# Attention with causal softmax, one core: weighted sums taken one key tile at a time, and part of the softmax denominators added up by VectorE

## What is computed

```
q = (x @ Wq.T + bq).reshape(b, l, h, hd).transpose(0, 2, 1, 3)      # k and v alike
scores = jnp.einsum('bhqd,bhkd->bhqk', q, k) / math.sqrt(hd)
scores = jnp.where(causal, scores, -jnp.inf)
att = jax.nn.softmax(scores, axis=-1)
out = jnp.einsum('bhqk,bhkd->bhqd', att, v)
return out.transpose(0, 2, 1, 3).reshape(b, l, d) @ Wo.T + bo
```

## Time and profile before

| what | value |
|---|---|
| median of 3 runs | 2973.25 us (2972.68 to 2973.93) |
| the profiled execution: its own time, and its span | 2975.39 us, 2972.8 us |
| TensorE busy, whole span | 2809.0 us (94%) |
| weight loads busy | 2017.9 us (68%) |
| VectorE busy | 1477.6 us (50%) |
| ScalarE busy | 1050.1 us (35%) |
| GpSimd busy | 1282.0 us (43%) |

### The profile page before, as it was taken

The page is one execution under the profiler, slowest core; times in us unless marked ns, Lnnn a source line. Parts: engine busy times, 40 slices in busy tenths (PEclk is TensorE's granted clock), DMA queues, the critical chain, the costliest instruction groups (busy, mean ns, idle before and its releaser), DMA issues. The chain is left out here.

```text
span 2972.8 us, 42529 instructions
## 1 busy us (share of the span) xinstructions
PE 2809.0 (94%) x16692; PEld 2017.9 (68%) x16692; DVE 1477.6 (50%) x3069; ACT 1050.1 (35%) x1446; POOL 1282.0 (43%) x672
## 2 busy tenths in 40 slices
PE   4999999999999999799999999999999968999998
PEld 2888888888888888555555555555555536888886
DVE  4232223222312222366666666666666626777775
ACT  1322321131213111255555555555555541212121
POOL 2322332242225111367777777777777741212110
PEclk8999999999999999799999999999999988999998
DMA  7444343333336544445455545555545235454541
GB/s 245 168 165 165 136 180 130 114 139 145 135 140 192 185 171 164 122 103 117 118 118 119 116 112 118 115 117 119 117 115 118 73 119 159 129 169 128 168 126 61
DMA packets 153999, 404.91 MB, mean 136 GB/s; under 512 B 21820, under 2 KB 57076, under 8 KB 152776
## 3 DMA queue, kind: packets, MB, share of 16 engines
q1 hardware_dynamic: 123480, 292.05, 28.9%
q10 hardware_dynamic: 30320, 110.15, 16.6%
HBM read 270.41 MB, written 131.20 MB: 135 GB/s over the span
## 5 line engine op out<-in xcount | busy, mean ns | idle before, releaser
L1087 ACT ACTIVATE prob<-ps_s 128x1024 f32<-128x1024 f32 (+3 forms) x768 | 598.5, 812 | 474.2 <-PE ps_s L1206 393.3
L787 PE MATMUL ps_u<-h_hi,w_hi 128*128 128x512 f32 x1536 | 611.9, 398 | 2.0 <-POOL h_lo L555 2.0
L787 PE MATMUL ps_u<-h_lo,w_hi 128*128 128x512 f32 x1536 | 600.7, 391 | 0.0
L787 PE MATMUL ps_u<-h_hi,w_lo 128*128 128x512 f32 x1536 | 599.5, 390 | 0.0
L1043 POOL TENSOR_TENSOR added<-added,prob 128x2048 f32<-128x2048 f32 (+1 forms) x128 | 550.0, 4297 | 10.7 <-ACT prob L1087 10.5
L549 POOL TENSOR_TENSOR w_lo<-w_raw,w_hi 128x1024 fp32r<-128x1024 f32 x93 | 222.7, 2395 | 473.0 <-ACT w_hi L617 473.0
L678 DVE SCALAR_TENSOR_TENSOR qk_lo<-ps_u,bias_col,qk_hi 128x512 fp32r<-128x512 f32 x128 | 96.0, 750 | 578.9 <-ACT qk_hi L593 578.9
L1130 DVE TENSOR_REDUCE part_high<-ps_r 128x1 f32<-128x512 f32 x496 | 329.9, 686 | 85.7 <-PE ps_r L1176 77.8
L1126 DVE CUSTOM_DVE_ANT_0 ps_r<-ps_r,row_mask 128x384 f32<-128x384 f32 (+1 forms) x500 | 309.1, 632 | 81.1 <-PE ps_r L1176 69.2
L1176 PE MATMUL ps_r<-k_st,q_st 96*128 96x512 f32 (+1 forms) x1008 | 323.3, 374 | 18.8 <-DMA v_sb<-v_tok 9.0
L787 PEld LDWEIGHTS ps_u<-h_lo,w_hi 128*128 128x128 f32 x1536 | 288.7, 188 | 61.9
(11 more groups left out here) (193 smaller groups left out, 3417.3 us busy)
## 6 DMA issues: line engine op xcount, KB each, us to landing
w_raw<-w_cols SPq DMA_DIRECT2D x72, 512.0 KB, 6.3
qk_split<-qk_hi SPq DMA_DIRECT2D x64, 512.0 KB, 2.6
qk_split<-qk_lo SPq DMA_DIRECT2D x64, 512.0 KB, 4.0
q_st<-qk_split ACTq DMA_DIRECT2D x60, 512.0 KB, 7.6
k_st<-qk_split ACTq DMA_DIRECT2D x60, 512.0 KB, 13.7
xn<-in_L_attn_x SPq DMA_DIRECT2D x8, 2048.0 KB, 12.8
v_tok<-v_out SPq DMA_DIRECT2D x32, 512.0 KB, 4.4
wm<-in_L_wmod SPq DMA_DIRECT2D x8, 2048.0 KB, 8.0
```

What stands on the lines that cost most here:

```text
L787: last = nc.tensor.matmul(ps_u[u % 2][:], w[:, m, k], h[:, k, tok], start=k == 0 and j == 0, stop=k == KT - 1 and j == 2)
L1087: nc.scalar.activation(prob[:, buffer_of(t, k), 2 * pair:2 * pair + 2, off:], ps_s[pair][:, :, off:], ACT.Exp, scale=SCALE).then_inc(exp_d ...
```

## The change

There are four parts.

1. `weigh` takes one step k instead of two. In the slots 2 to 5 the first step of the pair now stands behind the second pair of scores (`rest(t, p, 0)`), and the second at the end of the slot (`rest(t, p, 1)`). In slot 0 the steps 8 and 9 of the block before stand in the middle and `sum_high` at the end; in slot 1 the steps 10 and 11 and then `sum_low` stand at the end.
2. DVE adds the low half's steps into `low_total`, three instructions to a block (`add_low`), behind the second, fourth and sixth of its rows (`LOW_AT`). `sum_low` multiplies `low_total` (384 columns) and the first 128 columns of step 8 by ones.
3. `added` is one buffer instead of two. POOL's first add of a block waits for `sum_high` of the block before and for that block's three `low_added`.
4. ACT copies `ps_o` out before the first exponents of the next block, and the low half's before its sum. `SHARE` goes from (2, 2, 1, 1, 1) to (2, 1, 2, 1, 1).

```diff
-    SHARE = (2, 2, 1, 1, 1)
+    SHARE = (2, 1, 2, 1, 1)
...
                 if k == 1:
-                    if t > 1:
-                        pool.wait_ge(sum_done, sums_upto["sum", t - 2, 1])
+                    if t > 0:
+                        pool.wait_ge(sum_done, sums_upto["sum", t - 1, 1])
+                        pool.wait_ge(low_added, LOW_ADDS * t)
...
+            def add_low(t, i):
+                k = LONG + 1 + i
+                if i == 0:
+                    if t > 0:
+                        dve.wait_ge(sum_done, sums_upto["sum", t - 1, 0])
+                else:
+                    dve.wait_ge(low_added, LOW_ADDS * t + i)
+                dve.wait_ge(masked, masked_upto(t, k))
+                cols = slice(offset(k), BANK)
+                so_far = prob[:, buffer_of(t, LONG), :, cols] if i == 0 else low_total[:, :, cols]
+                nc.vector.tensor_tensor(low_total[:, :, cols], so_far, prob[:, buffer_of(t, k), :, cols], ALU.add).then_inc(low_added, 1)
...
-                pe.wait_ge(masked, masked_upto(t, NSTEP - 1))
-                for k in range(LONG, NSTEP):
-                    off = offset(k)
+                pe.wait_ge(masked, masked_upto(t, LONG))
+                pe.wait_ge(low_added, LOW_ADDS * (t + 1))
+                for total, cols in ((low_total[:], slice(P, BANK)), (prob[:, buffer_of(t, LONG)], slice(0, P))):
...
+            def rest(t, p, half):
+                if p >= HOPS:
+                    weigh(t, 2 * (p - HOPS) + half)
+                elif t > 0 and (p, half) == (0, 0):
+                    weigh(t - 1, LONG)
+                    weigh(t - 1, LONG + 1)
+                elif t > 0 and (p, half) == (0, 1):
+                    sum_high(t - 1)
+                elif t > 0 and (p, half) == (1, 1):
+                    weigh(t - 1, LONG + 2)
+                    weigh(t - 1, LONG + 3)
+                    sum_low(t - 1)
...
                         scores(t, 2 * p + n // 2, n % 2)
+                        if n == 1:
+                            rest(t, p, 0)
                     pass_1(turns[4])
-                    if p >= HOPS:
-                        weigh(t, p - HOPS)
-                    elif t > 0:
-                        (sum_high if p == 0 else sum_low)(t - 1)
-                        weigh(t - 1, PAIRS - HOPS + p)
+                    rest(t, p, 1)
```

More of the change, by code:

```diff
@@ L927, in attend @@
         prob = sb("prob", [P, PBUF, HG, BANK])
-        added = [sb(f"added{i}", [P, HG, BANK]) for i in range(2)]
+        added = sb("added", [P, HG, BANK])
+        low_total = sb("low_total", [P, HG, BANK])
         ones = sb("ones", [P, HD])
@@ L943, in attend @@
         added_up, sum_done, sum_copied = sem("added_up"), sem("sum_done"), sem("sum_copied")
+        low_added = sem("low_added")
         att_stored = [sem(f"att_stored{i}") for i in range(QC)]
@@ L1029, in add @@
             def add(t, k):
-                total, off = added[t % 2], offset(k)
+                total, off = added, offset(k)
                 if k < FIRST:
@@ L1078, in exponents @@
                 if before >= 0:
-                    act.wait_ge(weighed, before // 2 + 1)
+                    act.wait_ge(weighed, before + 1)
                     kb = before % NSTEP
@@ L1154, in _ @@
                             max_all(use[1])
+                    if t > 0 and n in LOW_AT:
+                        add_low(t - 1, LOW_AT.index(n))
+                for i, n in enumerate(LOW_AT):
+                    if t > 0 and n >= len(strewn(t)):
+                        add_low(t - 1, i)
+            for i in range(LOW_ADDS):
+                add_low(NG - 1, i)
         @block.tensor
@@ L1208, in scores, with weigh @@
                 last.then_inc(score_done, 1)
-            def weigh(t, p):
-                if 2 * p == 0 and t > 0:
+            def weigh(t, k):
+                if k == 0 and t > 0:
                     pe.wait_ge(o_copied, 2 * t)
-                if 2 * p == 0 and t == 0:
+                if k == 0 and t == 0:
                     pe.wait_ge(qkv_loaded[0], loads_upto(0))
-                if 2 * p == LONG:
+                if k == LONG:
                     pe.wait_ge(o_copied, 2 * t + 1)
-                if 2 * p < FIRST:
-                    pe.wait_ge(exp_done, 2 * (NSTEP * t + 2 * p + 2))
-                else:
-                    pe.wait_ge(masked, masked_upto(t, 2 * p + 1))
-                for k in (2 * p, 2 * p + 1):
-                    ch, j = steps[k]
-                    off, end = offset(k), j == (ch + 1) * CT - 1
-                    for h in range(HG):
-                        part = slice(h * HD, (h + 1) * HD)
-                        last = nc.tensor.matmul(ps_o[part, off:], v_sb[t % SLOTS][:, j, part], prob[:, buffer_of(t, k), h, off:], start=j == 0, stop=end)
+                if k < FIRST:
+                    pe.wait_ge(exp_done, 2 * (NSTEP * t + k + 1))
+                else:
+                    pe.wait_ge(masked, masked_upto(t, k))
+                ch, j = steps[k]
+                off, end = offset(k), j == (ch + 1) * CT - 1
+                for h in range(HG):
+                    part = slice(h * HD, (h + 1) * HD)
+                    last = nc.tensor.matmul(ps_o[part, off:], v_sb[t % SLOTS][:, j, part], prob[:, buffer_of(t, k), h, off:], start=j == 0, stop=end)
                 last.then_inc(weighed, 1)
                 if end:
-                    pe.wait_ge(weighed, PAIRS * t + p + 1)
+                    pe.wait_ge(weighed, NSTEP * t + k + 1)
                     pe.sem_inc(o_done, 1)
@@ L1236, in sum_low @@
                 bank_free(use)
-                pe.wait_ge(masked, masked_upto(t, NSTEP - 1))
-                for k in range(LONG, NSTEP):
-                    off = offset(k)
+                pe.wait_ge(masked, masked_upto(t, LONG))
+                pe.wait_ge(low_added, LOW_ADDS * (t + 1))
+                for total, cols in ((low_total[:], slice(P, BANK)), (prob[:, buffer_of(t, LONG)], slice(0, P))):
                     for h in range(HG):
-                        last = nc.tensor.matmul(bank_of(use)[h * HD:(h + 1) * HD, off:], ones[:], prob[:, buffer_of(t, k), h, off:], start=k == LONG, stop=k == NSTEP - 1)
+                        last = nc.tensor.matmul(bank_of(use)[h * HD:(h + 1) * HD, cols], ones[:], total[:, h, cols], start=cols.start > 0, stop=cols.start == 0)
                 last.then_inc(sum_done, 1)
@@ L1249, in sum_high @@
                 for h in range(HG):
-                    nc.tensor.matmul(bank_of(use)[h * HD:(h + 1) * HD, :], ones[:], added[t % 2][:, h], start=True, stop=False)
+                    nc.tensor.matmul(bank_of(use)[h * HD:(h + 1) * HD, :], ones[:], added[:, h], start=True, stop=False)
                 for k in range(ADDS + 1, LONG):
@@ L1269, in _ @@
                         scores(t, 2 * p + n // 2, n % 2)
+                        if n == 1:
+                            rest(t, p, 0)
                     pass_1(turns[4])
-                    if p >= HOPS:
-                        weigh(t, p - HOPS)
-                    elif t > 0:
-                        (sum_high if p == 0 else sum_low)(t - 1)
-                        weigh(t - 1, PAIRS - HOPS + p)
-            for p in range(PAIRS - HOPS, PAIRS):
-                (sum_low if p == PAIRS - 1 else sum_high)(NG - 1)
-                weigh(NG - 1, p)
+                    rest(t, p, 1)
+            weigh(NG - 1, LONG)
+            weigh(NG - 1, LONG + 1)
+            sum_high(NG - 1)
+            weigh(NG - 1, LONG + 2)
+            weigh(NG - 1, LONG + 3)
+            sum_low(NG - 1)
 def finish(nc, s):
```

15 lines of the change are left out of this document (8 added, 7 removed).

## The result

The changed kernel takes 2954.26 us (median of 4 runs, 2951.61 to 2954.96), the kernel before 2973.59 us beside it (2972.68 to 2974.79): ratio 0.9931, 95% interval 0.9918 to 0.9944. The direction is as forecast, and the time lies in the range. But 19 us were gained where 46 were forecast.

The account below looks back on a forecast made before the run. TensorE was taken as the bound, busy 35.5 of 36.7 us a block but losing waits to ACT and DVE. The terms summed to -1.50 us a block, -46 us over 31 blocks, so 2927 us; range 2888 to 2965.

Parts of the forecast that it names:

- the fifth: DVE's adds in slot 0 delay the bank `sum_high` needs: new wait 0.65 us a block, ends 0 and 3.
- Two rows of 0.5: DVE's two rows between first and second add in slot 0, reckoned at 0.5 us each, ending at 4.35 us.
- Step 1: The low half's sum on TensorE shrinks from 2.18 to 0.88 us: gain 1.30 us a block.
- Step 2: Five more 32-column groups on TensorE cost 1.5 us a block; its own-matmul wait ahead of `sum_low` adds 0.1.
- step 3: TensorE's scores wait less for ACT's exponents: about 2.0 us a block recovered, ends 0.8 and 3.1.
- step 4: TensorE's waits for DVE outside slot 0: 0.45 of some 0.7 us a block recovered, ends 0 and 0.7.
- Step 6: POOL's first add moves from 5.7 to about 7.9 us into the block, covered by 2.96 us of POOL idling.
- the third rival: DVE adds meeting POOL adds choke the rows: +1.0 us a block, 3004 us; chance 0.11.
- the second: Rival: width changes eat the gain, only 0.8 to 1.3 us of waits recovered; 2955 to 2980 us, chance 0.18.
- The first: Rival: waits vanish almost whole, slot 2 too, none at `sum_high`; -2.9 us a block, 2883 us; chance 0.14.

Follow-up runs that it names:

- order alone: The changed kernel without DVE's adds and with the low half's sum over all four steps as before: 2966.29 us, ratio 0.9975.
- no adds: The changed kernel without DVE's three adds, `sum_low` reading step 8 alone for all 512 columns: 2926.55 us, ratio 0.9845.
- with pairs: The changed kernel with adds behind DVE's rows 2, 5 and 7, and pairs of steps again in slots 2 to 5: 2926.22 us, ratio 0.9839.
- the first experiment: The kernel before with only DVE's adds and the short low sum; order, pairs of steps, `SHARE` and ACT's copies as before: 2998.28 us, ratio 1.0082.
- sum-first order: The changed kernel with adds behind rows 2, 5 and 7, and `sum_low` ahead of the weighted sums of steps 10 and 11: 2937.56 us, ratio 0.9875.

## Why the forecast was right in direction and wrong in size

The forecast's sum and what was measured, in us to a block. Two kernels lie on the way from before to changed (order alone, then no adds, which has the shorter sum as well), so the measured terms add up to the whole difference:

| step | forecast | measured | from the table of slots |
|---|---|---|---|
| 1, the shorter sum | -1.30 | -1.29 | order alone to no adds |
| 2, five groups | +1.50 | +1.55 | five times 0.31 |
| 2, wait for the own matmul | +0.10 | +0.30 | slot 1, before to order alone |
| 3 and 4, waits recovered | -2.45 | -2.28 | the rest of before to order alone (-0.43) |
| 5, adds on DVE | +0.65 | +0.95 | no adds to changed |
| sum | -1.50 | -0.77 | -0.72 by the period |

**The step that failed** is the fifth, "the adds on DVE", with about +0.3 the largest miss of a single term (+0.28 by the period). Its mechanism and place are right: a wait ahead of `sum_high` for the bank of one DVE row, and the same kernel gains 23.6 us when one add is moved behind that row. The size was wrong because the reckoning moved TensorE's arrival by the group of steps 8 and 9, but not the row behind that group which DVE needs. "Two rows of 0.5" contained an idle 0.35 us. The steps 2 to 4 together miss by more than the fifth, 0.42: the new order was to bring 0.85 us and brought 0.43, for the two reasons that follow (the wait for the own matmul, and the waits recovered).

**Step 1** held. The sum is 1.00 us long rather than 0.88, and still the group with the sum first is 1.29 us shorter. **Step 2** held within 0.1 for the groups. The wait for the own last matmul took 0.30 us instead of 0.10; it was sized from a place where a width change hides part of it (0.18 idle in the earlier trace rows) and shows 0.33 us idle inside a group. The Trainium skill (TensorEngine Tiling (Array Packing), Key Properties) says that a change of tiling mode drains TensorE; by that rule, the trace agrees: 0.31 to 0.33 us for each group.

**Steps 3 and 4** came to -2.28 us together instead of -2.45, but in other places and from other causes. With 0.31 us for each added group taken off, from before to the order alone the waits recovered are 0.37 us in slot 0, 0.67 in slot 2, 0.14 in slot 3, 0.72 in slot 4 and 0.37 in slot 5. The forecast had 0.6 us at the scores behind the loads' issue (it calls that place slot 2, rightly slot 3), and slot 3 gave almost nothing. Slot 2 ahead of it is 0.36 us shorter than before, so it is likely that part of the wait only moved there; that is not shown by itself. About 0.3 of the rest in slot 4 came with the new `SHARE`, and the early copies are worth 0.3 in slot 3; these two were measured in other surroundings than the changed kernel, so they do not add up exactly. How the recovered waits split between ACT (step 3) and DVE (step 4) is not measured; the chain of waits has -1.95 us for ACT.

**Step 6** held. POOL's first add came 0.65 us later than forecast, and its cover shrank to 0.20 us; no mask was late for it. POOL was idle from 1817.8 to 1825.95 us, in which all three adds of that block lie (1819.06 to 1824.9). So no DVE add met a POOL add there, and the third rival's price had no occasion. The Trainium skill (SBUF — State Buffer, Who interferes with whom) says that two such instructions lock each other out; by that rule, the trace agrees in one place of the changed kernel, behind the last block, where the first add starts beside POOL's last masks and takes 2.68 us. In the 31 blocks ahead of it this add takes 1.75 to 1.76.

```profile
2389.96 1.80 POOL L1030 TENSOR_SCALAR_AFFINE_SELECT prob<-prob 128x512 f32<-128x512 f32 x3
```

```profile
2390.70 2.68 DVE L1162 TENSOR_TENSOR low_total<-prob 128x1536 f32<-128x1536 f32 x1 [26.28 <-POOL prob L1030]
```

It ends 1.62 us after POOL does, about the length that it has alone. That happens once in the whole execution.

**The rivals.** The time lies just inside what was given to the second (2950 to 2980), but not for its reason: it wanted 0.8 to 1.3 us of recovered waits, and over 2 were. In the slots 2 to 5 alone it is right: there the width changes and slot 3's wait ate what single steps recovered (21.5 us with them, 21.4 with pairs). The third was right in this, that the adds by themselves choke the rows and make the kernel slower (the first experiment). The first fell: in the order of the changed kernel slot 3 did not recover until the loads went to SP. The forecast was a small difference of large terms, 3.75 us of gains less 2.25 us of costs, and three terms that were each off by 0.2 to 0.3 us, all on one side, halved it. A sum of that kind should have had a range reaching further toward no change, and the second rival more chance.

What stays open: whether the sum-first order gains, how the recovered waits split between ACT and DVE, and why slot 3 loses next to nothing to the issue with pairs (5.19 us, and 5.17 with the loads on SP) and 0.81 us with single steps.

## What to carry over

When work is moved to an engine that feeds the bounding one, write both engines' queues out side by side to the wanted buffer, and shift the inputs of the second by what was put ahead of them on the first; then place the new instruction behind the row whose buffer is wanted next, which here turned 19 us of gain into 42. Look for what else stands in the queue of the engine that is waited for: seven DMA issues on ACT cost 0.8 us to a block in the changed order, more than the whole rearrangement brought. A recovered wait counts only once the next one on the way is priced: what slot 2 gained, slot 3 lost. A sum in which large terms cancel needs a range made of all their errors at once.

## What the runs showed of the chip that was not expected

- A group of 32-column matmuls between full-width ones costs 0.31 to 0.33 us beyond its columns, whether it has 512 or 1024 columns to a head.
- TensorE's wait for its own last matmul idles it 0.33 us inside a group of 32-column matmuls, and 0.18 us where a change to full width follows it. To have it inside costs 0.29 to 0.30 us more.
- Moving seven DMA issues from ACT's queue to SP's is worth 23 us of 2931 with single steps. On SP the issue takes as long, 4.3 us from 1809.54 to 1813.86, but nothing urgent stands behind it. The first of its rows on SP's timeline:

```profile
1809.54 2.29 SPq L975 DMA_DIRECT2D slot_q<-qk_split  x3
```

- A copy of 0.60 us on ACT, placed behind the exponents of step 0 instead of ahead of them, made TensorE lose 3.35 us to a block: 2.0 us of waiting, and 1.3 us behind it. The granted clock fell to 0.50 there in the block shown, after 1.96 us without a matmul, and the group is as slow in 16 of 26 blocks.
- A DVE add of two SBUF inputs took 2.68 us instead of 1.75 beside POOL's masks.
